# Eight attention heads: four of a head's five count products on GpSimd, two of VectorE's steps moved among the scores, and two edits in the stages around them

## The reference, cut to what matters

```
h = (x @ W).reshape(n, heads, out_c)
e = leaky_relu(al_s[src] + al_d[dst], 0.2)
m = segment_max(e, dst);  ex = exp(e - m[dst])
out = segment_sum(h[src] * ex / (z[dst] + 1e-16), dst) + bias
x = elu(out)                  # then a second layer: one head of 768 features
```

## Time and profile before

| | us |
|---|---|
| median of three runs (lowest to highest) | 1436.75 (1436.01 to 1437.41) |
| the profiled execution, its own time | 1437.73 |
| its span in the trace | 1436.0 |

### The profile page before, as it was taken

The page is one execution under the profiler, slowest core; times in us unless marked ns, Lnnn a source line. Parts: engine busy times, 40 slices in busy tenths (PEclk is TensorE's granted clock), DMA queues, the critical chain, the costliest instruction groups (busy, mean ns, idle before and its releaser), DMA issues.

```text
span 1436.0 us, 22503 instructions
## 1 busy us (share of the span) xinstructions
PE 1367.7 (95%) x7784; PEld 1274.6 (89%) x7784; DVE 762.8 (53%) x1818; ACT 441.9 (31%) x936; POOL 559.0 (39%) x629
## 2 busy tenths in 40 slices
PE   5999999999999999999999999999998999988997
PEld 3676999999999999999999999999888887878874
DVE  6876755224544356474232434765375504599644
ACT  1564521102010000100110222255574424467631
POOL 8000324324243525343442423143433463548830
PEclk9999999999999999999999999999999999998999
DMA  3101111113333223242211211221101310200001
GB/s 117 55 29 34 39 34 50 50 34 109 105 107 105 67 89 115 72 131 68 67 55 45 68 53 46 61 83 57 56 23 39 107 53 17 82 18 1 1 11 54
DMA packets 57804, 86.49 MB, mean 60 GB/s; under 512 B 6468, under 2 KB 54459, under 8 KB 57584
## 3 DMA queue, kind: packets, MB, share of 16 engines
q1 hardware_dynamic: 45204, 65.82, 15.8%
q10 hardware_dynamic: 12504, 19.36, 4.4%
HBM read 83.24 MB, written 1.92 MB: 59 GB/s over the span
## 4 chain that ended last, share of the span: by engine, by line
PE 76%; DVE 13%; ACT 4%; issue 3%; POOL 3%; DMA 1%; DVEq 0%; SPq 0%; ACTq 0%; POOLq 0%
PE psum L2487 13%; PE psum L2491 13%; PE psum L2490 13%; PE psum L2504 7%; PE psum L2507 7%; PE psum L2988 4%; DVE max_scratch L2189 3%; PE psum L2636 3%; PE psum L2561 2%; POOL w_lo L919 2%; PE psum L2530 1%; PE psum L2533 1%; PE psum L2476 1%; DVE more_tiles L2233 1%; DVE score_tiles L2233 1%
## 5 line engine op out<-in xcount | busy, mean ns | idle before, releaser
L2487 PE MATMUL psum<-w_lo,xT_hi 128*125 128x384 f32 (+4 forms) x1110 | 377.4, 340 | 3.3 <-POOL w_lo L919 1.8
L2491 PE MATMUL psum<-w_hi,xT_hi 128*125 128x384 f32 (+4 forms) x1110 | 373.4, 336 | 0.0
L2490 PE MATMUL psum<-w_hi,xT_lo 128*125 128x384 f32 (+4 forms) x1110 | 373.3, 336 | 0.0
L906 POOL CAST w_hi<-w_raw 128x384 fp32r<-128x384 f32 x190 | 105.2, 553 | 569.7 <-PE psum L2491 466.0
L1093 ACT ACTIVATE h_hi<-psum 125x384 fp32r<-125x384 f32 (+1 forms) x120 | 59.1, 492 | 529.3 <-PE psum L2491 524.9
L1739 DVE TENSOR_TENSOR h_lo<-psum,h_hi 125x384 fp32r<-125x384 f32 (+1 forms) x120 | 66.9, 558 | 288.0 <-ACT h_hi L1093 287.2
L2487 PEld LDWEIGHTS psum<-w_lo,xT_hi 128*125 128x125 f32 (+1 forms) x1110 | 205.9, 186 | 6.1 <-POOL w_lo L919 3.4
L908 POOL TENSOR_TENSOR w_lo<-w_raw,w_hi 128x384 fp32r<-128x384 f32 x190 | 201.2, 1059 | 15.2
L2490 PEld LDWEIGHTS psum<-w_hi,xT_lo 128*125 128x125 f32 (+1 forms) x1110 | 206.4, 186 | 0.4
L2491 PEld LDWEIGHTS psum<-w_hi,xT_hi 128*125 128x125 f32 (+1 forms) x1110 | 206.0, 186 | 0.0
L2504 PE MATMUL psum<-h_lo,adjacency 125*125 125x384 f32 (+3 forms) x600 | 203.5, 339 | 2.1 <-issue 1.9
(11 more groups left out here) (350 smaller groups left out, 2272.2 us busy)
## 6 DMA issues: line engine op xcount, KB each, us to landing
w_raw<-weights_dram SPq DMA_DIRECT2D x296, 192.0 KB, 2.4
score_w_raw<-weights_dram ACTq DMA_DIRECT2D x58, 192.0 KB, 2.8
x_nat<-x_dram SPq DMA_DIRECT2D x1, 1875.0 KB
x_residual<-x_dram SPq DMA_DIRECT2D x5, 375.0 KB
score_a_rows<-L_gnn_a_src_dram ACTq DMA_DIRECT2D x8, 192.0 KB, 3.3
score_a_rows<-L_gnn_a_dst_dram ACTq DMA_DIRECT2D x8, 192.0 KB, 4.5
out_dram<-x_residual SPq DMA_DIRECT2D x4, 375.0 KB
rgcn_bias<-rgcn_bias_dram SPq DMA_DIRECT2D x1, 1125.0 KB
```

The lines of the kernel that those rows point to most:

```text
L906: nc.gpsimd.tensor_copy(mem.wh[:, slot, :], mem.raw[:, raw_slot, :]).then_inc(w_hi_ready, 1)
L2487: ins = nc.tensor.matmul(o, h, wl, start=(j == 0), stop=False, skip_group_check=True)
L2490: nc.tensor.matmul(o, l, wh, start=False, stop=False, skip_group_check=True)
L2491: ins = nc.tensor.matmul(o, h, wh, start=False, stop=stop and j == k - 1, skip_group_check=True)
```

## The change

In the order of the diff: Q1 sends its columns at block 22, not 16. A fourth place for counts, `counts_late`, lies where a mask of earlier layers was. `LATE` goes from 3 to 4, so that GpSimd makes the products of tiles 1 to 4 and ScalarE limits these four; tile 0 stays with VectorE. The adds of the last bias row move to a place ahead of GpSimd's first head, with their load (from ScalarE's queue, into `par0`, with a semaphore of its own) moved ahead of Q2. GpSimd's order in a head becomes: first product of head h+1, `unit_sum(h-1)`, the other three products, `unit_bias(h)`. VectorE's one `finish` goes into `head_scores`, after the second score, and `columns` go ahead of the third score.

```diff
 PAIR_EVENTS = {3: (("scores", 0),), 6: (("row", 0),), 16: (("send", 0),)}
+LONG_EVENTS = {3: (("scores", 0),), 6: (("row", 0),), 22: (("send", 0),)}
...
-Q1 = Attention(Q0, 1, D, K8, PIECES, True, BASE_L2B, True, PAIR_EVENTS, {})
+Q1 = Attention(Q0, 1, D, K8, PIECES, True, BASE_L2B, True, LONG_EVENTS, {})
...
+        self.counts_late = at("counts_late", [128, N], F32, ah + 86464)
...
+        last_bias_loaded = sem("last_bias_loaded")
...
-        LATE = 3
+        LATE, COLUMNS_AT, FINISH_AT = 4, 2, 1
...
-            late_counts = [mem.counts_f[0:BP, 0, :], mem.counts_f[0:BP, 1, :], mem.par0b[0:BP, 0:N]]
+            late_counts = [mem.counts_late[0:BP, :], mem.counts_f[0:BP, 0, :], mem.counts_f[0:BP, 1, :], mem.par0b[0:BP, 0:N]]
             for i, t in enumerate(late_counts):
                 nc.gpsimd.tensor_copy(t, mem.ctot[0:BP, NB - LATE + i, 0:N]).then_inc(rows_added, 1)
             pool.wait_ge(rows_added, 1 + NB + LATE)
-
-            def late_products(h):
-
-                for i, counts in enumerate(late_counts):
+            pool.wait_ge(last_bias_loaded, 16)
+            pool.wait_ge(xT_lo_ready, T_Q[2] + UNITS)
+            for m in range(NB):
+                r = mem.xres[0:BP, m, :]
+                nc.gpsimd.tensor_tensor(r, r, mem.par[0][0:BP, 0:D], ALU.add).then_inc(res_biased, 1)
+
+            def late_products(h, a, e):
+
+                for i, counts in list(enumerate(late_counts))[a:e]:
...
-            late_products(0)
+            late_products(0, 0, LATE)
             for h in range(LAST):
-                late_products(h + 1)
-                unit_bias(h)
+                late_products(h + 1, 0, 1)
                 if h:
                     unit_sum(h - 1)
+                late_products(h + 1, 1, LATE)
+                unit_bias(h)
             unit_sum(LAST - 1)
             split_to(NCHUNKS)
-
-            pool.wait_ge(params_loaded, 16 * 9)
-            pool.wait_ge(cols_ready, Q3.head0 + 1)
-            for m in range(NB):
-                r = mem.xres[0:BP, m, :]
-                nc.gpsimd.tensor_tensor(r, r, mem.par[1][0:BP, 0:D], ALU.add).then_inc(res_biased, 1)
...
             load_row("L3_gnn_b1", par[1], D)
+            load_part("L3_gnn_b2", par[0], 0, D, last_bias_loaded)
...
                 source_below(h, NB - LATE)
-                for k in range(NB - LATE, NB):
+                source_exp_below(h, NB - LATE)
+                source_below(h, NB - LATE + 1)
+                for k in range(NB - LATE + 1, NB):
                     if k + 1 < NB:
                         source_below(h, k + 1)
                     source_exp_below(h, k)
...
-            load_row("L3_gnn_b2", par[1], D)
             feature_product(Q3)
...
             def head_scores(h):
 
                 for k in range(NB):
-                    if k == NB - 1 and h + 2 < HEADS3:
+                    if k == COLUMNS_AT and h + 2 < HEADS3:
                         columns(Q2, h + 2)
                     score(Q2, h, k)
+                    if k == FINISH_AT:
+                        for i in range(NB - LATE):
+                            finish(Q2, h, i)
...
                 if h:
                     head_z(h - 1)
-                for k in range(NB - LATE):
-                    finish(Q2, h, k)
                 if h + 3 < HEADS3:
                     maxima(Q2, h + 3)
```

## The result

The changed kernel takes 1456.99 us (median of four runs, 1455.6 to 1458.0) against 1436.67 for the kernel before (also four runs): 1.0141 times as long, 95% interval 1.0123 to 1.0158. The profiled execution took 1455.6, with a span of 1453.9. The forecast was 1459.4.

The account below looks back on a forecast made before the run. VectorE was taken to bound the kernel before, the new order the changed one. Heads +24.1, last bias -3.7 and Q1's columns +2.3 sum to +22.7 on the median 1436.75: 1459.4 us, range 1444 to 1465.5.

Parts of the forecast that it names:

- The bound and the exclusion: Heads: VectorE sets the pace at 11.4 us; its two-SBUF-operand steps and GpSimd's instructions exclude one another, whole instructions at a time.
- The term that was too large: Heads 3 to 5: finish and column steps meet GpSimd's unbroken run, so each such head lasts 15.3 us.
- The other heads: Heads without that full collision: head 0 at 14.8 us, head 1 at 10.7, head 2 at 11.2, head 6 at 10.9.
- the tail: End of the heads, from head 7's first score to TensorE's last sum: 16.8 us.
- the hold: Heads: GpSimd's instructions block VectorE's column steps at the shared SBUF port; heads cost +24.1 with it, +9.6 without.
- The rival in which the columns slip through: Heads: column steps find gaps in GpSimd's run, ScalarE's 11.2 sets the pace; +8.2 in all, 1445 us; chance 0.17.
- Part 2: Last bias: its adds leave Q3, finishes are no longer held, TensorE's wait falls from 3.42 to 1.3; -3.7 us.
- Part 3: Q1's columns sent at block 22: the removed wait returns at the feature reads, 1.14 growing to 4.2; +2.3 us.
- the fall of the clock behind the wait: Q1, after the longer wait at the feature reads: TensorE's clock may fall, raising the cost from +1.4 to +3.1.

Follow-up runs that it names:

- columns_free: Changed kernel with the four column steps of heads 2 to 7 reading one operand from PSUM instead of SBUF: 1446.73 us, 1.0069 of before.
- bias_behind: Kernel before, last bias's adds left in the fourth network's second layer but waiting for VectorE's fifth finish instead of its columns: 1433.58 us, 0.9975.
- bias_ahead: Kernel before with only the five adds of the last bias and their load moved ahead of GpSimd's first head: 1435.49 us, 0.9986 of before.
- after_bias_behind: Changed kernel with the last bias's five adds put behind VectorE's fifth finish in the fourth network's second layer: 1456.97 us.
- after: The changed kernel with all edits of the change, against the kernel before: 1456.99 us, 1.0141 times as long.

## Why the prediction was right, step by step

- *The bound and the exclusion.* In heads 3 to 5 the mechanism held instruction by instruction. One reading was loose: GpSimd's idle 1.90 in the earlier trace rows ends with an Exp of ScalarE, and only ScalarE's 2.96 in the earlier trace rows ends with VectorE; the bound stays the same. Counted from the strip Exp's end (about 1300.84), the finish was to end at 5.1 and ends at 5.1; then forecast and, in brackets, measured: the first column step at 6.55 (6.4), the second at 8.2 (7.9), the third and fourth at 9.6 (9.0), the third score at 10.4 (9.9), the next strip Exp at 15.3 (14.4).
- *The term that was too large* is that head: 15.3 forecast, 14.4 measured, three times, 2.6 of the 3.5 by which the heads were overestimated. I had let each column step delay GpSimd by 0.2; a product with a column step ahead of it takes 1.50 and without one 1.50, so only the finish delays it. And limits and Exps come at 4.5, not 4.8, a head.
- *The other heads.* First score to first score: head 0 14.5 (14.8 forecast), head 1 10.8 (10.7), head 2 10.9 (11.2), head 6 10.6 (10.9), the tail 16.8 (16.8). Head 0 came out close by another sequence, which is luck in part: the finish was to get in ahead of an add and the first column step to wait for that add; instead the finish waited for the last add (2.39) and the first step for the product (1.46). The third score came 7.4 after the first and not 8.2, and a wait of 0.55 for TensorE ahead of the next head, which the sum did not have, took most of that back. The product from `counts_late` was priced at 1.27 and took 1.52; in heads 3 to 5 that cost nothing, since GpSimd rests after it.
- *What the hold is worth.* The forecast split +24.1 into 14.5 for the hold and 9.6 for the rest. columns_free splits the measured +21.1 (the sums of the table; +20.6 from first score to last sum) into 11.0 and 10.1. The rival in which the columns slip through was put at 1445; with the hold taken away it is 1446.7. The exclusion of the column steps thus decided between that rival and the forecast. The exclusion is also what the Trainium skill, "SBUF — State Buffer", section "Who interferes with whom", says of a VectorE instruction with two SBUF inputs; the trace agrees: 1.12 to 1.42 with two, 0.15 to 0.17 with one, in the same place.
- *Part 2*, -3.7: bias_behind alone gives -4.0, and behind the wait of 1.42 the clock of the changed kernel stays at 1.00 (1413.1 to 1420.0), as the forecast had it. The price in the heads, which the forecast had inside head 0's 14.8, is 2.7 by bias_ahead, so in the kernel before the move was worth 2.1 of the 4.0; in the changed kernel it came out equal to adds behind the fifth finish (after_bias_behind).
- *Part 3*, +2.3: alone +2.4, and the agreement is partly luck. The wait came out as forecast (4.4 against 4.2) and the later send cost 1.2 to 1.3 (1.4 forecast). But the fall of the clock behind the wait, for which the sum had some 0.9, cost nothing, and a second fall, which I had not seen coming, cost 0.5 to 1.5 in its place. In the profiles, from a point ahead of all edits (TensorE's wait of 2.04 to 2.05 near 1084) to head 0's kept row, the seven kernels with the send at 22 take 181.6 to 183.2 (after 181.9), the six others 179.8 to 180.8 (before 180.8); so the profiled execution of after, where the second fall cost 0.5, shows less than half of the 2.4, which is part of why it came out below the forecast.

## What to carry to other kernels

Where two engines exclude one another by whole instructions, tiny steps are the ones to place with care: four steps on 125 x 5 values took 3.9 us a head because three of them met a long GpSimd instruction, and they took 0.5 to 0.6 with an operand in PSUM or in a gap of GpSimd. Before moving work to an engine with spare time, lay out in one row, from the event that releases it, what that engine then does without a gap, and see who must pass through it: the gap that is given up may have been carrying someone else's steps. A step that nobody waits for yet (the bias adds) was better held back behind the work that it would hold than moved ahead to another idle gap: 4.0 against 2.1 us in the kernel before. In the changed kernel the two places came out equal.

## What the runs showed of the hardware that I had not expected

- A second fall of TensorE's clock follows the one behind the long wait at the features, some 85 to 100 us later, in all seven kernels that send the columns at block 22 (from 1228 in after and columns_free, from between 1240 and 1244 in the five others), and in none of the six that send them at 16 or 19, although those have the same waits there (0.84 at 1227, 0.85 and 1.29 around 1240). From VectorE's reciprocal near 1190, ahead of this second fall, to head 0's kept row the six kernels without it take 75.2 to 75.3, the two in which it comes at 1228 take 75.7 to 75.8, and the five others 76.7 to 76.9: it costs 0.5 or 1.5. What ties it to the first, or to the later send, is not settled.
- Where nothing holds it, GpSimd's product on 125 x 625 values takes 1.27 to 1.32 with the counts in `counts_wide` (2.53 to 2.64 for two) and 1.49 to 1.53 with them in `par0b` or `counts_late`, in every kernel here. The difference, about 0.2, goes with the place of the counts; each place is tied to its source tiles (`counts_wide` to tiles 2 and 3), so which of the two it is, and why, was not tried.
